# Row buffers in another order, the scale factor g applied by two engines, and dot products over more steps, in a recommendation kernel

## What is computed

```python
h = jnp.concatenate([q1, q2], axis=1) @ w5 + b5        # q1, q2: two attention poolings of x, 1024 x 50 x 300
f6 = h @ w6 + b6
iu, ju = jnp.triu_indices(E, k=1)                      # E = 300: 44850 pairs
g = (v @ v.T)[iu, ju]
cross = h[:, iu] * h[:, ju] * g                        # 1024 x 44850
f7 = cross @ w7 + b7                                   # w7 is 44850 x 300
out8 = jnp.concatenate([f6, f7], axis=1) @ w8 + b8
return jnp.einsum('bu,bku->bk', out8, label_embedding) # label_embedding: 1024 x 200 x 300
```

## Time and profile before

| | |
|---|---|
| median of 3 runs | 1860.07 us (1859.95 to 1860.88) |
| the profiled execution | 1859.29 us, its span 1857.5 us |
| PE / DVE / ACT busy | 1615.5 us (87%) / 1479.9 us (80%) / 919.1 us (49%) |
| matmuls of line 600 | 5616, of 2808 pairs of pair tile and batch tile |
| chain that ended last | PE bank L600 64%, ACT stream L747 6%, DMA wring 5%, DVE junk L819 3% |
| moved by DMA | 617 MB, mean 332 GB/s |

### The profile page before, as it was taken

How to read it: one execution, slowest core, us unless ns; L and a number is a source line. 1 busy time by engine, 2 the same in 40 slices (tenths; PEclk the granted TensorE clock), 3 DMA queues, 4 the chain that set the end, 5 groups by cost and what they waited for, 6 DMA issues and landing times.

```text
span 1857.5 us, 25035 instructions
## 1 busy us (share of the span) xinstructions
PE 1615.5 (87%) x7142; PEld 1165.1 (63%) x7142; DVE 1479.9 (80%) x5516; ACT 919.1 (49%) x2844; POOL 33.4 (2%) x62
## 2 busy tenths in 40 slices
PE   0569999999999999997999999999999999998300
PEld 0236677776777767774777777767777777666200
DVE  8898986863699989967899976758777677498996
ACT  4433376654564636463465634434444444200698
POOL 0000000000000000000000000000000000000000
PEclk9889999999999999998999999999999999999655
DMA  7669867767789898998989999999999899899895
GB/s 279 237 256 352 344 245 260 264 222 278 263 301 420 324 401 335 389 334 308 381 300 407 352 394 386 364 294 403 355 342 342 305 385 354 272 420 421 338 417 244
DMA packets 139215, 617.00 MB, mean 332 GB/s; under 512 B 16432, under 2 KB 43693, under 8 KB 106181
## 3 DMA queue, kind: packets, MB, share of 16 engines
q1 hardware_dynamic: 105157, 368.23, 52.8%
q10 hardware_dynamic: 31744, 244.16, 34.0%
q0 software_dynamic: 2176, 3.01, 0.5%
HBM read 611.55 MB, written 3.79 MB: 331 GB/s over the span
## 4 chain that ended last, share of the span: by engine, by line
PE 72%; DMA 7%; ACT 7%; DVE 7%; SPq 4%; issue 2%; ACTq 0%; POOL 0%; DVEq 0%; POOLq 0%
PE bank L600 64%; ACT stream L747 6%; DMA wring<-in_w7p 5%; DVE junk L819 3%; PE bank L549 3%; SPq L438 3%; PE bank L563 2%; DMA sring<-hrows 2%; DVE stream L935 1%; PE bank L612 1%; PE bank L610 1%; DVE cring L917 1%; DVE cring L905 1%; ACT absjunk L663 1%; SPq L444 0%
## 5 line engine op out<-in xcount | busy, mean ns | idle before, releaser
L600 PE MATMUL bank<-wring,cring 128*128 128x300 f32 (+1 forms) x5616 | 1448.0, 419 | 52.8 <-DVE cring L917 19.6
L600 PEld LDWEIGHTS bank<-wring,cring 128*128 128x128 f32 (+1 forms) x5616 | 1064.1, 191 | 420.8 <-DVE cring L905 30.4
L738 ACT ACTIVATE wring<-wring,gcol 128x300 f32<-128x300 f32 x1237 | 565.1, 533 | 608.8 <-PE bank L600 340.3
L935 DVE SCALAR_TENSOR_TENSOR stream<-stream,out 128x300 f32<-128x300 f32 x1335 | 546.4, 466 | 0.9 <-DMA stream<-in_label 0.2
L917 DVE TENSOR_TENSOR cring<-lefts,sring 128x1024 f32<-128x1024 f32 (+2 forms) x309 | 368.3, 1193 | 205.1 <-PE bank L600 202.6
L819 DVE SCALAR_TENSOR_TENSOR junk<-stream,ubc 128x300 bf16<-128x300 f32 x896 | 364.2, 466 | 4.3 <-DMA stream<-in_x 4.2
L663 ACT ACTIVATE absjunk<-stream 128x300 bf16<-128x300 f32 x448 | 196.3, 440 | 50.3 <-PE bank L600 48.6
L747 ACT ACTIVATE stream<-stream 128x300 f32<-128x300 f32 x265 | 115.5, 441 | 0.1
L549 PE MATMUL bank<-stream,wts 128*32 128x300 f32 x896 | 66.6, 453 | 55.8 <-DVE small L861 55.8
L935 DVE DVE_READ_ACCUMULATOR stream<-stream,out 128x1 f32 x1335 | 109.9, 82 | 0.0
L905 DVE SCALAR_TENSOR_TENSOR cring<-lefts,gcol,sring 128x128 f32<-128x128 f32 x334 | 95.2, 348 | 16.8 <-PE bank L600 15.7
(11 more groups left out here) (62 smaller groups left out, 247.7 us busy)
## 6 DMA issues: line engine op xcount, KB each, us to landing
stream<-in_label SPq DMA_DIRECT2D x320, 750.0 KB, 8.2
wring<-in_w7p ACTq DMA_DIRECT2D x184, 1200.0 KB, 8.4
stream<-in_x SPq DMA_DIRECT2D x64, 1050.0 KB, 12.6
sring<-hrows SPq DMA_DIRECT2D x152, 256.0 KB
wring<-in_w7p ACTq DMA_DIRECT2D x9, 1050.0 KB, 8.6
wring<-in_w7p ACTq DMA_DIRECT2D x9, 600.0 KB, 7.5
lefts<-hrows SPq DMA_DIRECT2D x48, 64.0 KB, 2.6
sring<-hrows SPq DMA_DIRECT2D x32, 88.0 KB
```

What stands on the lines that cost most here:

```text
L600: mm = pe.matmul(acc[b % 4][:, 0:E], cring[0:rows, p % CSLOTS, b % 2, j0 + j, :], w, start=(p == BEGIN[b] and j == 0), stop=(p == END[b] - ...
L738: ins = nc.scalar.activation(w, w, ACT.Copy, scale=gcol[:, t:t + 1])
L935: ins = nc.vector.scalar_tensor_tensor(out=row_in, in0=row_in, scalar=1.0, in1=out8[:, m % 4, :], op0=ALU.mult, op1=ALU.mult, accum_out=sc ...
```

## The change

It does four things.

1. **Order of the buffers** (`ORDER`): A0 A1 D0 A2 own0 A3 D1 A4 own1 A5 D2 A6 own2 A7, then the eight B. In a cycle the units are now: A0 0 to 7, A1 8 to 14, D0 15 and 16, A2 17 to 23, own0 24, A3 25 to 31, D1 32 and 33, A4 34 to 40, own1 41, A5 42 to 48, D2 49 and 50, A6 51 to 57, own2 58 (one pair tile), A7 59 to 65, B 66 to 90. The rule for loading stays: the buffer after the next two goes into the slot that is free. `SHIFT` follows the start of A5 and is 42, and there are 406 steps.
2. **g where one tile runs** (`folded`): ACT scales w7 at every step now, but leaves out the last two pair tiles of a unit in steps 0 to 41 and the last one in steps 364 to 405. For those DVE multiplies by g as before; the other pair tiles are one TENSOR_TENSOR. PE waits for ACT's scaling at every step (`w7_ready`), and where DVE takes a share for the load as well. ACT scales the units of steps 0 and 1 before step 0.
3. **Dots**: half tile 3 over 24 steps in place of 12 (14 of its 56 rows ahead of step 0 in place of 28), the next ones later and over other lengths. The x loads follow the table, so they move: groups of four at steps -20, 0, 1, 25, 41, 57, 67, 77, 87, 124, 147 ... in place of -20, -13, 1, 13, 31, 50, 61, 72, 84, 121, 144 ... The loads for the slots of half tile 1 (`x_free`) come at step 0 behind the first two right buffers and the left pieces; at step -13 before.
4. **Labels**: `EARLY_ROWS` is 80, so 64 chunks come after the last step, 51 of them shared.

```diff
+ORDER = (("A", 0), ("A", 1), ("D", 0), ("A", 2), ("own", 0), ("A", 3), ("D", 1), ("A", 4), ("own", 1), ("A", 5),
+         ("D", 2), ("A", 6), ("own", 2), ("A", 7)) + tuple(("B", k) for k in range(NB))
...
-    SHIFT = next(k for k, u in enumerate(UNITS) if u[1] == 6)
+    SHIFT = FIRST_USE[KINDS.index(("A", 5))]
...
+    def folded(p):
+
+        n = UNITS[p % NU][3]
+        return 0 if len(live(p)) == 2 or n == 1 else min(2, n - 1) if p < NU else 1
...
-    DOTS = [(-34, -27), (-27, -20), (-20, -6), (-6, 6), (6, 24), (24, 43), (43, 54), (54, 65), (65, 77), (77, 89),
-            (100, 114), (123, 137), (146, 160), (169, 183), (192, 206), (215, 229)]
+    DOTS = [(-34, -27), (-27, -20), (-20, -6), (-6, 18), (18, 34), (34, 50), (50, 60), (60, 70), (70, 80), (80, 92),
+            (103, 117), (126, 140), (149, 163), (172, 186), (195, 209), (218, 232)]
...
-    EARLY_ROWS = 65
+    EARLY_ROWS = 80
...
+    def x_free(s):
+
+
+        return 0 if s == 1 else DOTS[s][1] + X_FREE
...
-                if SHIFT <= p < SHIFT + BOTH:
-                    pe.wait_ge(w7_ready, p - SHIFT + 1)
-                else:
+                pe.wait_ge(w7_ready, p + 1)
+                if folded(p):
                     pe.wait_ge(w7_in[n_block % WSLOTS], 16 * (n_block // WSLOTS + 1))
...
-                for t in range(UNIT_TILE[u], UNIT_TILE[u + 1]):
+                for t in range(UNIT_TILE[u], UNIT_TILE[u + 1] - folded(p)):
...
-                    if SHIFT <= q + AHEAD < SHIFT + BOTH:
+                    if q + AHEAD < POS:
                         w7_scale(q + AHEAD)
...
+                if q == -1:
+                    for p in range(AHEAD):
+                        w7_scale(p)
...
-                    b = tiles[0]
-                    for j in range(j0, j0 + n):
+                    b, whole = tiles[0], n - folded(p)
...
+                    in0 = (one.unsqueeze(1).to_broadcast([rows, whole, P]) if one is not None
+                           else cut(sring, (nb + 1) % SSLOTS, j0, whole))
+                    nc.vector.tensor_tensor(cut(cring, p % CSLOTS, j0, whole), in0, cut(sring, nb % SSLOTS, j0, whole),
+                                            ALU.mult).then_inc(c_ready, 1)
```

139 lines of the change are left out of this document (69 added, 70 removed).

## The result

The changed kernel takes 1882.88 us (median of 4 runs, 1881.29 to 1887.74) against 1860.01 us for the kernel before on the same chip. The ratio is 1.0127, with a 95% interval of 1.0108 to 1.0146. It is slower by 23 us, where 14 us less were forecast; it lies outside the range of 1811 to 1864 us as well. The profiled execution took 1883.7 us, with a span of 1881.9 us.

A forecast was written before the change was run, and what follows sets the result against it. PE was taken to bound the middle, with 69 us of standing at known places. Terms of -2, -6, -33, +11.5, +22.4, -3.5, +1 and -4.4 gave -14 us, so 1846 us, range 1811 to 1864.

The forecast's parts named there:

- Start: Fewer row dots on DVE ahead of step 0 shorten PE's wait at the first matmul; gain 2 us.
- Tile 0 alone: Steps 0 to 42: DVE's delays go, w7 loads get worse; standing 14 us for 20.3, gain 6.
- Ends of the cycles: PE's stands at the four cycle ends go, as own and D buffers move away; gain 33 us.
- fourth rival: Own loads in small pieces behind x groups still cost half of the 33 us at cycle ends: 1862 us, 10%.
- A buffers behind own ones with two tiles: A3, A5 and A7, issued only two steps before use after own units, land late with two tiles: 11.5 us lost.
- The seven other such places with two tiles: A loads after own units, two tiles running, no x group just ahead: 2 us of standing for all.
- Step 387: With tile 7 alone, A3's load stands behind label loads on SP's queue: 18.4 us of standing, 22.4 with slower clock.
- third rival: With tile 7 alone, A3 finds a shorter queue and stands 5 us in place of 22: 1829 us, 20%.
- Rest of tile 7 alone: Tile 7 alone apart from A3's wait: DVE quicker, label backlog gone, gain 3.5 us; ACT's scaling between loads costs 1.
- second rival: w7 loop through ACT: two blocks per landing and scaling, 6.3 us a block with tile 7 alone; 1874 us, 12%.
- The sign that I had named for being wrong here: Forecast wrong if DVE never waits for `sring` with tile 7 alone, or w7 blocks there come slower than every 5 us.
- Tail: ACT's chain after the last step has 10 rows fewer at 0.437 us a row: 4.4 us less.

## Why the prediction was wrong

Two steps failed. One is the 2 us for the right buffers behind own ones that have no x group just ahead, which cost 21 us in steps 130 to 224. The other is the price of ACT's scaling of w7, 1.5 us with tile 0 alone and 1 us with tile 7 alone, which came to 5.6 us and, with what ACT delayed for PE, to some 16 us in the rest of that stretch. Term by term, forecast and then trace:

- **Start, -2**: -3.5 in the trace. Right in sign; the first matmul moves more than that by itself.
- **Tile 0 alone, -6**: +0.7. Half of the step was right: DVE was relieved, and the dots without sharing bring 19.6 down to 14.7. The term that failed is "ACT's scaling stands between two loads ... I give it 1.5 us". Sharing costs 5.6 us there. I priced the scaling as time in the loop of loads, and not as a deadline two steps earlier for blocks that land just in time: with one step in place of two ACT's waits for w7 fall from 39.1 to 24.0 us and the kernel from 1882.9 to 1877.9.
- **Ends of the cycles, -33**: right, 34.0 to 0.4, and to at most 3.0 in every kernel with the new order. The fourth rival is refuted.
- **A buffers behind own ones with two tiles, +11.5 (bounds 0 and 25)**: +40.8, beyond the bound. Step 148 was sized at 6.5 and cost some 10 (7.75 and the lower clock). Step 57 was sized at 3 and cost nothing; no labels are loaded yet there. The failed term is "The seven other such places with two tiles have no x group just ahead; 2 us for all." They cost 21 us, at steps 133 and 224. I looked one step back. The group of step 124 was seven steps ahead of A5's load; behind it the small own loads held SP for 24.46 us, and the labels that came due meanwhile went out together ahead of A5. The issue time of a small load behind a full queue was in none of my rows, and I did not bound it. Another 5 us are DVE's wait for the x group of step 216 itself, for which the sum had no term.
- **Step 387, +22.4**: +7.3. The mechanism stands, DVE waiting once for `sring` ahead of the 26th unit. The size failed: A3 was used 18 us after its issue and not 28.3, and PE stood 5.90 us for it. ACT's scaling slowed PE down ahead of this place, so that the buffers were needed later; where VectorE multiplies by g, steps 388 and 389 stand 14 and 17 us in two kernels, closer to the forecast. The change's own figure is near the third rival's (5 us), but that came from a loss the rival did not have.
- **Rest of tile 7 alone, -2.5 with the scaling's +1**: +14. The failed step is again ACT. The term of 1 us for the scaling is the one that was mis-sized. The second rival had the loop through ACT, but priced it as two blocks for each landing, 33 us. What came was the turned f7 behind the scaling (9 us), which no text of mine named, and 5 us of pace. The sign that I had named for being wrong here came: the 21 blocks of the stretch took 124.6 us, one every 5.9 us and not every 5. Without the sharing the stretch stands 14 us beside steps 388 and 389 (30.9 less 17), for 16.4 before, as forecast; so the whole miss of this term is the sharing's. I listed what waits for ACT's scaling, but not what is queued behind it on ACT.
- **Tail, -4.4**: -2.2. ACT's chain is shorter by 2.2 us (two pieces of 102.38 and 2.19 us for 106.75). I counted ten rows, but the piece that sets the end lost only ten of its 489 instructions, five rows.
- **The sum**: the loss at the ends was right to a us, the new ones were low by some 37 us. Faster was called with 77%, and it is slower. The two faults are of one kind: a queue and an engine take things in order, and I looked only at the thing that was moved.

One slip in the sums changes nothing: 76.4 us for 32 steps are 2.39 us a step and not 2.35.

What stays open: how the 14 us of sharing in the pair with blocks of one unit divide between the product with w5 and the rest, since no kernel moved that eviction alone; how long an issue on SP takes for a given amount of loads ahead; and whether A5's delay is the labels' place in the queue or the bytes alone, since every kernel that took it away changed both.

## What to carry to other kernels

A reorder that takes buffers away from a crowded place is worth its gain only if every buffer keeps its lead in the new places; look back on the queue for a large group, here as far as ten steps, and not one, and give the ring one slot more in the same edit. A task given to an idle engine costs what stands behind it in that engine's order: its waits become the waits of all its later work, here an eviction that PE needed. A loss that is removed ahead of another can be given back there, so test a fix in the kernel where the other loss is gone.
